# Attention denominators moved directly behind the router logits in a fused graph-layer, linear-attention and expert kernel

## What is computed

```python
xn = _layernorm(x)
# graph layer: gather rows by edge, softmax over 4 heads, weighted sum
x = x + gnn(xn, edges) + mix(xn)
x = x + ffn(_layernorm(x))

def mix(x):                       # linear attention, 8 heads of 32 channels
    q = x @ Wq;  Q = elu(q) + 1;  K = elu(x @ Wk) + 1;  v = x @ Wv
    KV = K^T v ;  Z = 1 / (Q . sum(K) + eps)      # Z: one denominator for each row and head
    msg = layernorm((Q KV Z) @ Wm)
    h = relu(concat(x, msg) @ W1) @ W2
    return x + layernorm(h)

def ffn(x):                       # shared MLP and 4 experts, the 2 best by the router
    shared = mlp(x, sW1, sW2, sW3)
    gates = softmax(x @ gW + gb)                  # the router logits
    return shared + sum over the top 2 of weight * expert_mlp(x, eW1, eW2, eW3)
```

## Time and profile before

| | us |
|---|---|
| three runs, median (lowest to highest) | 1364.05 (1363.18 to 1364.38) |
| the profiled execution, its own time | 1364.58 |
| its span | 1362.8 |
| TensorE busy in the span | 1326.4 (97%) |
| VectorE, ScalarE, GpSimd busy | 1032.9, 739.3, 823.9 |

### The profile page before, as it was taken

How to read it: one execution, slowest core, us unless ns; L and a number is a source line. 1 busy time by engine, 2 the same in 40 slices (tenths; PEclk the granted TensorE clock), 3 DMA queues, 4 the chain that set the end, 5 groups by cost and what they waited for, 6 DMA issues and landing times.

```text
span 1362.8 us, 26649 instructions
## 1 busy us (share of the span) xinstructions
PE 1326.4 (97%) x8932; PEld 1150.0 (84%) x8932; DVE 1032.9 (76%) x2617; ACT 739.3 (54%) x1339; POOL 823.9 (60%) x816
## 2 busy tenths in 40 slices
PE   6999999998999999999999999999999999999997
PEld 5999999876888888888888888888888888888885
DVE  6867677877787777877778777877778777787774
ACT  4555556334655655556554555545565455655655
POOL 5777666746655675556655667556665566655540
PEclk9999999998999999999999999999999999999999
DMA  5787767422211221112211122122221222211001
GB/s 175 253 277 236 244 203 255 130 58 70 68 34 54 76 75 49 49 55 76 72 41 58 57 76 70 30 69 59 76 68 31 66 63 76 68 31 53 23 16 31
DMA packets 71737, 121.81 MB, mean 89 GB/s; under 512 B 38035, under 2 KB 42768, under 8 KB 71705
## 3 DMA queue, kind: packets, MB, share of 16 engines
q1 hardware_dynamic: 55704, 108.00, 25.0%
q0 software_dynamic: 16000, 13.43, 4.5%
HBM read 69.47 MB, written 51.70 MB: 89 GB/s over the span
## 4 chain that ended last, share of the span: by engine, by line
PE 86%; DVE 5%; ACT 3%; issue 2%; POOL 1%; DMA 1%; DVEq 1%; SPq 0%; POOLq 0%; ACTq 0%
PE psum L228 26%; PE psum L229 25%; PE psum L230 25%; PE psum L434 5%; DVE qf L1494 2%; PE psum L700 1%; ACT s_hi L965 1%; PE psum L617 1%; PE psum L507 1%; ACT relu L964 1%; PE psum L514 1%; PE psum L715 1%; POOL xg L1771 1%; POOL ag L1773 1%; DMA xb<-in_x 0%
## 5 line engine op out<-in xcount | busy, mean ns | idle before, releaser
L1777 POOL TENSOR_TENSOR s_lo<-relu,s_hi 128x500 fp32r<-128x500 f32 (+1 forms) x46 | 83.0, 1804 | 149.8 <-ACT s_hi L965 144.5
L228 PE MATMUL psum<-w_hi,h_hi 128*125 128x256 f32 x600 | 170.8, 285 | 0.5 <-DVE h_lo L1555 0.4
L230 PE MATMUL psum<-w_hi,h_lo 128*125 128x256 f32 x600 | 168.4, 281 | 0.0
L229 PE MATMUL psum<-w_lo,h_hi 128*125 128x256 f32 x600 | 168.2, 280 | 0.0
L1777 POOL TENSOR_TENSOR h_lo<-relu,h_hi 128x1000 fp32r<-128x1000 f32 x50 | 124.8, 2497 | 49.1 <-ACT h_hi L965 49.0
L1771 POOL DMA_INDIRECT xg<-table_xt,idx x100 | 126.6, 1266 | 39.0 <-issue 37.9
L1773 POOL DMA_INDIRECT ag<-table_al,idx x100 | 121.7, 1217 | 30.5 <-issue 30.5
L228 PE MATMUL psum<-z_hi,w_hi 128*128 128x500 f32 x300 | 122.0, 407 | 3.3 <-DVE z_lo L1463 2.3
L228 PE MATMUL psum<-xT_hi,w_hi 128*128 128x500 f32 x300 | 120.0, 400 | 0.4 <-ACT row_n L889 0.4
L229 PE MATMUL psum<-xT_lo,w_hi 128*128 128x500 f32 x300 | 117.3, 391 | 0.0
L230 PE MATMUL psum<-xT_hi,w_lo 128*128 128x500 f32 x300 | 117.3, 391 | 0.0
(11 more groups left out here) (266 smaller groups left out, 4348.3 us busy)
## 6 DMA issues: line engine op xcount, KB each, us to landing
xb<-in_x SPq DMA_DIRECT2D x50, 448.0 KB
xT_hi_table<-x1T_hi SPq DMA_DIRECT2D x25, 500.0 KB
xT_lo_table<-x1T_lo SPq DMA_DIRECT2D x25, 500.0 KB
xT_hi<-xT_hi_table SPq DMA_DIRECT2D x25, 500.0 KB, 3.9
xT_lo<-xT_lo_table SPq DMA_DIRECT2D x25, 500.0 KB, 4.9
table_xt<-xts SPq DMA_DIRECT2D x25, 455.0 KB
out<-xmid SPq DMA_DIRECT2D x24, 448.0 KB
xb<-in_x SPq DMA_DIRECT2D x50, 52.0 KB
```

The costliest lines, as they stand in the source:

```text
L228: pe.matmul(out, wh, xh, start=first, stop=False)
L229: pe.matmul(out, wh, xl, start=False, stop=False)
L230: return pe.matmul(out, wl, xh, start=False, stop=last)
L1777: ptt(out, src, hi, ALU.subtract).then_inc(S[done], 1)
```

## The change

The denominators move on TensorE from behind the experts to directly behind the router logits. For that, the query product and its two VectorE steps and the exponential move ahead of W1 on the message, to banks 2 and 3, and the first expert layers take banks 4, 6, 7 and 1. `p2_logits` is the former inner function `logits_of_z`. The branches on `a`, `b`, `c` are written out, since all turns that use the function took the same ones. The spread of the reciprocals (`p2_expand`) and all that comes after it keep their places and banks.

```diff
+E1_BANKS, Q_BANK = (4, 6, 7, 1), 2
...
-            def w2_pair(i, pair, c):
+            def w2_pair(i, pair):
 
                 if pair == 0:
-                    if due(2 * i):
-                        pe.wait_ge(S["h_lo"], 2 * i)
-                if c:
-                    if pair == 1:
-                        pe.wait_ge(S["e1_relu"], 4 * (i - 2) + 1)
-                    elif due(2 * (i - 1)):
-                        pe.wait_ge(S["s1_relu"], 2 * (i - 1))
+                    pe.wait_ge(S["s1_relu"], 2 * (i - 1))
+                else:
+                    pe.wait_ge(S["e1_relu"], 4 * (i - 1))
...
+            def p2_logits(i):
+
+                pe.wait_ge(S["zf"], i - 1)
+                for c in range(CK):
+                    for j in range(T):
+                        last = pe.matmul(psum[j * QUAD:(j + 1) * QUAD, 1, 0:R], gate_w[:, c, :], tile(zf, c, j),
+                                         start=c == 0, stop=c == CK - 1)
+                last.then_inc(S["lg_mm"], 1)
...
+                if not x_ahead:
+                    hidden_of_old_x()
+                if own_q:
+                    pe.wait_ge(S["out"], i - 2)
+                    p2_q(i, par, Q_BANK)
+                pe.wait_ge(S["mT"], i)
...
+                pe.wait_ge(S["zT"], i - 1)
+                pe.wait_ge(S["h_relu"], 4 * (i - 1) + 2)
+                hidden("sW1", 0, 0, 5, zT).then_inc(S["s1_mm"], 1)
+                p2_logits(i)
+                p2_den(i, Q_BANK)
+                hidden("sW1", 0, 1, 0, zT).then_inc(S["s1_mm"], 1)
+                pe.wait_ge(S["h_relu"], 4 * (i - 1) + 4)
+                for e in range(EXPERTS):
+                    if e == 1:
+                        pe.wait_ge(S["s1_relu"], 2 * (i - 2) + 1)
+                        pe.wait_ge(S["lg"], i - 1)
+                        pe.transpose(psum[0:R, 5, 0:P], logitsT[:], ident[:]).then_inc(S["lt_mm"], 1)
+                    hidden("eW1", 2 * e, 0, E1_BANKS[e], zT).then_inc(S["e1_mm"], 1)
+                pe.wait_ge(S["h_lo"], 2 * i)
+                for pair in range(2):
+                    w2_pair(i, pair)
...
+                relu_split(relu[0][:, 0, :], h_hi[:, 0, :], 4, h_bias[:, 0:1], 4 * (i - 1) + 1, "h_mm", "h_relu")
+                if own_q:
+                    p2_exp(i)
+                act.wait_ge(S["zt"], i - 1)
+                act.activation(z_hi[:], colT(0, 2), ACT.Copy).then_inc(S["z_hi"], 1)
...
+                if a and q_at is None:
+                    feature_low(i, Q_BANK)
+                    feature_high(i, Q_BANK)
                 if c:
                     if due(i - 1):
                         dve.wait_ge(S["z_hi"], i - 1)
                     tt(z_lo[:], colT(0, 2), z_hi[:], ALU.subtract).then_inc(S["zT"], 1)
                 if b:
                     residual(i - 1, 1 - par, (1, 2, 3))
-                if a and q_at is None:
-                    feature_low(i)
-                    feature_high(i)
...
+                if a:
+                    one_over_den(i, Q_BANK)
                 if c:
                     soft_chain_in(i, par, a, c)
                     dve.drain()
                     compare(i)
                     soft_chain_out(i, a, c)
                     top_weights(i)
-                if a:
-                    one_over_den(i)
```

More of the change, by code:

```diff
@@ L601, in second_experts, with phase2 @@
                 last.then_inc(S["e2_mm"], 1)
-            def phase2(i, par, a=True, b=True, c=True, own_q=True, x_ahead=False):
+            def phase2(i, par, own_q=True, x_ahead=False):
                 xT, mT, zT = (xT_hi[par], xT_lo[par]), (mT_hi, mT_lo), (z_hi, z_lo)
                 xT_old = (xT_hi[1 - par], xT_lo[1 - par])
[L607 to L619, removed]
                 def hidden_of_old_x():
@@ L625, in hidden_of_old_x @@
                     w1_part(0, 3, 7, xT_old).then_inc(S["xT_free"], 1)
[L627 to L644, removed]
@@ L645, in phase2 @@
[L645 to L647 removed]
+                if x_ahead:
+                    hidden_of_old_x()
+                pe.wait_ge(S["y"], i - 1)
+                transposes(row_n, 0, "mt", "m_norm", T * (i - 1))
+                if not x_ahead:
+                    hidden_of_old_x()
+                if own_q:
+                    pe.wait_ge(S["out"], i - 2)
+                    p2_q(i, par, Q_BANK)
@@ L648, in phase2 @@
+                pe.wait_ge(S["mT"], i)
+                for o in range(4 if x_ahead else 2):
+                    w1_part(1, o, 4 + o, mT).then_inc(S["h_mm"], 1)
+                transposes(row_z, 0, "zt", "z_norm", T * (i - 2))
+                if not x_ahead:
                     for o in range(2, 4):
                         w1_part(1, o, 4 + o, mT).then_inc(S["h_mm"], 1)
[L650 to L661, removed]
@@ L662, in phase2 @@
-                if a:
[L663 to L692, removed]
-                    for q in range(2):
[L694 to L724, removed]
@@ new lines, in phase2 @@
+                pe.wait_ge(S["h_lo"], 2 * i)
+                for pair in range(2):
+                    w2_pair(i, pair)
+                pe.wait_ge(S["gate_rows"], i - 1)
+                pe.transpose(psum[:, 5, 0:R], flat(scale_rows), ident[0:R, 0:R]).then_inc(S["scale_t"], 1)
+                p2_expand(i)
+                pe.wait_ge(S["s1_lo"], i - 1)
+                hidden("sW2", 0, 0, 4, (s1_hi, s1_lo)).then_inc(S["s2_mm"], 1)
+                for q in range(2):
+                    second_experts(i, q)
@@ new lines, in phase2 @@
+                pe.wait_ge(S["scaleT"], i - 1)
+                pe.wait_ge(S["s2_relu"], i - 1)
+                for q in range(2):
+                    last = pe.matmul(colT(4 + q), gate_sel[:, q, :], scaleT[:], start=True, stop=True)
+                last.then_inc(S["gb"], 1)
+                p2_m(i)
+                pe.wait_ge(S["e2g"], 2 * (i - 1))
+                w1_part(0, 0, 4, xT)
+                w1_part(0, 1, 5, xT)
+                pe.wait_ge(S["s2_lo"], i - 1)
+                pe.wait_ge(S["e2_relu"], 2 * (i - 1))
@@ new lines, in phase2 @@
+                for j in range(T):
+                    out = rowt(2, j)
+                    pe.matmul(out, scaleT[:, j * R:(j + 1) * R], out_bias[:], start=True, stop=False)
+                    split_mm(pe, out, (s2_hi[:, j * R:(j + 1) * R], s2_lo[:, j * R:(j + 1) * R]),
+                             (wslice(w_hi, "sW3", 0), wslice(w_lo, "sW3", 0)), False, False)
+                    if j == 0:
+                        pe.wait_ge(S["e2_lo"], i - 1)
+                    for q in range(2):
+                        last = split_mm(pe, out, (tile(h_hi, q, j), tile(h_lo, q, j)),
+                                        (wslice(w_hi, "eW3", q), wslice(w_lo, "eW3", q)), False, q == 1)
@@ L726, in expert @@
+                last.then_inc(S["out_mm"], 1)
             def expert(e, bank):
```

111 lines of the change are left out of this document (35 added, 76 removed).

## The result

Six runs of the changed kernel took 1351.52 us (1351.16 to 1353.01), six of the kernel before on the same chip 1364.22 (1362.92 to 1364.83). The ratio is 0.991 (95% interval 0.9900 to 0.9921): 12.7 us faster. The forecast was 8 us, and the result is 1.5 us under the low end of its range. The span went from 1362.8 to 1349.6.

The account below looks back on a forecast made before the run. The prediction took TensorE's own work as the bound. Its terms, -7.0 - 1.3 + 0.3 = -8.0 us, took the profiled 1364.58 to 1356.6, and 1356.0 for the median, which lies 0.53 lower; range 1353 to 1360.

Parts of the forecast that it names:

- Part 1, the join: Denominators directly behind the logits on TensorE: 0.44 us in place of 0.76, -7.0 us over turns 3 to 24.
- The first rival: Joining the narrow blocks saves nothing, as each block keeps its 0.32 us: 1363.1 us, chance 0.07.
- the third (short supply): Instructions for the joined block come too slowly: 1388 us, or 1358.2 with a partial stumble; chance 0.05, shared with late `zT`.
- Parts 2 to 4: q ahead of W1 on the message, `zT` ahead of `sW1`, and waits further down: cost 0 each, `zT` at most +2.2 us.
- Part 5, the soft chain: VectorE's chain behind `one_over_den`: softmax's input ready at 762.8, earlier than the old 763.60, so cost 0.
- Part 6, the wait at the gates: TensorE's 0.17 us wait at the spread of the gates shrinks by 0.06 a turn: -1.3 us, bounds 0 and -2.6.
- The fourth rival: All of the 0.17 us wait at the spread of the gates goes, 0.11 more a turn: 1353.6 us, chance 0.04.
- Part 7, turn 2: W2's second pair waits 0.6 us in turn 2, less 0.32 for the join: +0.3 us, once.

Follow-up runs that it names:

- e8: The kernel after, with the denominators behind the second half of `sW1` and three quarters of GpSimd's addition to `base` behind its gathers; 1359.15 us.
- e5: The kernel after, with the sixteen logits matmuls made once more, unused, directly behind the denominators as a third joined narrow block; 1361.27 us.
- e10: The kernel after, with the logits made once more, unused, by themselves between the second half of `sW1` and the first expert; 1370.21 us.
- e2: The kernel after, with VectorE's reciprocals put back behind the soft chain and TensorE's join kept; 1412.21 us.
- e1: The kernel before, with VectorE's statistics of W2's first pair put behind the product with the reciprocals; 1358.35 us.
- e11: The kernel after, with VectorE's statistics of W2's first pair put behind the product with the reciprocals; 1351.93 us.
- e3: The kernel after, with the denominators put behind the second half of `sW1`, so that the narrow blocks stand apart; 1368.94 us.

## Why the prediction fell short

**Part 1, the join: right.** Forecast 0.32 us a turn, measured 0.33 in the traces, 0.32 by e8 and 0.33 by e5 against e10. The first rival (no saving) and the third (short supply) are refuted.

**Parts 2 to 4: right in the outcome.** None of q, `zT`, `zf` or `h_relu` makes TensorE wait. `z_lo` starts at 789.25, 11.17 us into the turn, and follows `feature_high` at once, as computed.

**Part 5, the soft chain: cost 0 is right, its working is not.** It put the softmax's input at 20.3 us into the turn, measured 23.4, and so gave the fourth ReLU 3 us more slack than it has. The chain was priced with its old durations at a new place, where GpSimd's instructions run. e2 shows what that is worth where the reciprocals stand behind it: 61 us more than the kernel after, 7 of them clock. With GpSimd's order as it is, only their place ahead of the chain makes the change a gain. That the cost came out as 0 in spite of the working was luck.

**Part 6, the wait at the gates: the step that failed.** The prediction said that `z_hi` "waits for that and for its four copies, which end at 770.87 + 1.10 = 771.97", let that bound the gain at 0.12 us and took 0.06. Measured is 0.22, 4.5 us in place of 1.3. The bound was wrong in two ways. First, the end of a recorded ACTIVATE is no bound for the next. In the rows above `z_hi` starts at 807.09, while the copies last until 806.08 + 1.11 = 807.19. The product's first half is over 0.11 us before that start, so the copies do hold the first half of `z_hi` now, but 0.10 us less than reckoned. Second, the working stopped at the first half of `z_hi`. The second half, with the ReLU pair and the spread of the gates behind it, starts 0.70 us behind the second half of the product before, after and in e1. By the mean of the turns 4 to 22, the first half of `z_hi` comes 0.16 us nearer to the spread of the reciprocals (1.46 to 1.29 us behind its start), the second 0.24 (2.04 to 1.81). What had held the product was the statistics ahead of it, and they do so no longer (e1, e11): it starts 0.51 us behind the spread (805.80 to 806.31) rather than 0.75 (770.63 to 771.38). And the true wait was 0.22 us, more than the 0.17 of the earlier trace rows; the ends of matmuls in the profile are modelled, which can account for the rest. The low bound of that part, -2.6, was thus too near as well. The fourth rival named this outcome with a chance of 0.04, at 0.11 more a turn, and missed the size.

**Part 7, turn 2:** +0.06 in place of +0.3, small. The new wait of W2's second pair for line 927 is there, at 0.2 us in place of 0.6.

The sum by the measured terms: 7.2 + 4.5 + 0.9 are the 12.6 us of the turns, against 8.3 forecast for them; turn 2 takes 0.06 off. The 0.9 of small shifts was not forecast. The spans differ by 13.3 us. The rest of that is 0.4 from turn 1 (30.0 to 30.7 us from run to run) and 1.2 from the first phase, which the change does not touch (277.6 to 279.4 from run to run), less the 0.9 behind turn 24.

## What to carry to other kernels

Where TensorE is the bound, look for narrow matmul blocks among wide ones and stand them side by side: here each return trip in width costs 0.33 us, and a joined block of sixteen only its own 0.45. Before moving a chain of small VectorE instructions, lay GpSimd's timeline beside its new place; here those with two SBUF inputs ended with the long GpSimd tensor instruction beside them. When a wait of TensorE is to be priced, follow the last arrival back through every instruction queued ahead of it, and don't take the recorded end of one ACTIVATE as the earliest start of the next. Before a difference outside the changed stretch is put down to a change, look at the granted clock there.

## What the runs showed of the hardware

- VectorE, 125x16 elements with two SBUF inputs: 184 ns alone, 2187 beside a GpSimd instruction of 2.39 us, all of it counted as busy. A busy VectorE at 82% can be one that stands still.
- The granted TensorE clock can fall to half for 3.4 us in the midst of a run. It cost 0.9 us behind turn 24 of the kernel after, and some 1.4 us in each of five turns of e2.
- ScalarE's ACTIVATEs overlap on record: line 914 starts at 808.25 and lasts 0.68, and line 915 starts at 808.83, 0.10 us before that end. The Trainium skill gives about 93 ns as the overlap of ACTIVATEs back to back (ScalarE: Activation LUTs, What ACT_TABLE_LOAD costs). The trace agrees: `z_hi` starts 0.09 us before the copies' end by the mean of the turns 4 to 22 of the kernel after.
- A turn can lose 0.65 us though TensorE's recorded starts run on in step where the loss begins (e3). It appears there only as later updates of semaphores, and then as a wait further on, at a line that the edit did not touch:

```profile
PE psum L661 <- ACT s_hi L915: 9.4, 16, 0.7
```
